# Last stage, slots with experts: TensorE sums the states behind both expert steps, VectorE reads the sums half a slot later, and the closing addition moves to the next slot

## The reference, cut to what matters

```python
x = x + _L1_attn_ref(_layernorm(x), ...)    # recurrence over 32 steps, 512 channels x 16 states
x = x + _L1_ffn_ref(_layernorm(x), ...)     # 8 experts, each 256 -> 512 -> 256
...
    h = dA * h + dBx                        # dA = exp(A * dt), dBx = dt * B_t * x_t
    y = jnp.einsum('bdn,bn->bd', h, C_t) + D * x_t
...
    y = y * jax.nn.silu(z)
    y = y @ out_proj_w.T + out_proj_b       # + residual, layernorm
...
    h = jax.nn.gelu(jnp.einsum('nd,edh->neh', xf, w1) + b1, approximate=False)
    y = jnp.einsum('neh,ehd->ned', h, w2) + b2
    out = (y * norm_g[:, None, None]).sum(axis=1)
```

## Time and profile before

| | us |
|---|---|
| median of 3 runs | 1709.85 (1709.10 to 1711.02) |
| the profiled execution's own time | 1710.99 |
| its span, first to last instruction | 1709.2 |
| last stage with units alone, to the first expert step | about 982 to 1184 |
| last stage, units and experts (40 slots) | about 1184 to 1552 |
| last stage, experts alone | about 1552 to 1704 |
| VectorE busy in the 368 us with both | 342.07 |
| TensorE busy in these 368 us | 311.80 |

### The profile page before, as it was taken

The page is one execution under the profiler, slowest core; times in us unless marked ns, Lnnn a source line. Parts: engine busy times, 40 slices in busy tenths (PEclk is TensorE's granted clock), DMA queues, the critical chain, the costliest instruction groups (busy, mean ns, idle before and its releaser), DMA issues. The chain is left out here.

```text
span 1709.2 us, 33886 instructions
## 1 busy us (share of the span) xinstructions
PE 1373.8 (80%) x12684; PEld 781.7 (46%) x12684; DVE 1221.7 (71%) x2296; ACT 1074.7 (63%) x1902; POOL 772.2 (45%) x842
## 2 busy tenths in 40 slices
PE   5999547978769977877783578995888888799898
PEld 4544223655444435555552223341444445446566
DVE  3599799962348856777765698989999899893100
ACT  1577345543354447777773367876988798894553
POOL 2255000000043434343430077767888788885433
PEclk8999767989869978888895789996999899899999
DMA  6398200000106757776732397877985475460000
GB/s 255 138 352 315 105 0 0 1 1 0 70 32 228 204 109 134 130 127 127 125 62 53 76 246 199 227 217 183 223 187 123 112 177 132 111 149 1 6 8 13
DMA packets 152695, 211.88 MB, mean 124 GB/s; under 512 B 107247, under 2 KB 112303, under 8 KB 139600
## 3 DMA queue, kind: packets, MB, share of 16 engines
q1 hardware_dynamic: 152532, 209.70, 47.5%
HBM read 154.85 MB, written 31.75 MB: 109 GB/s over the span
## 5 line engine op out<-in xcount | busy, mean ns | idle before, releaser
L2865 POOL TENSOR_TENSOR c_st<-c_st,c_c_rep 128x1024 f32<-128x1024 f32 x128 | 301.5, 2356 | 128.1 <-DVE c_st L2978 128.1
L2978 DVE TENSOR_TENSOR_SCAN c_st<-mf_dA,mf_u_ps 128x512 f32<-128x512 f32 x256 | 310.3, 1213 | 2.6 <-ACT mf_dA L3090 2.6
L2806 PE MATMUL mf_eh<-c_early,c_experts 128*128 128x512 f16 x768 | 197.3, 395 | 26.8 <-POOL c_early L2884 15.6
L2888 POOL TENSOR_TENSOR c_early<-c_early 128x512 f16<-128x512 f32 x128 | 149.1, 1166 | 112.0 <-ACT c_early L3107 111.9
L2827 PE MATMUL mf_ey<-c_experts,c_early 128*128 128x256 f16 x1536 | 192.7, 277 | 0.0
L2972 DVE TENSOR_TENSOR mf_u_ps<-c_st,mf_b_ps 128x512 f32<-128x512 f32 x256 | 177.6, 694 | 11.3 <-DVE c_st L2978 0.5
L2827 PEld LDWEIGHTS mf_ey<-c_experts,c_early 128*128 128x128 f16 x1536 | 152.3, 99 | 50.1 <-issue 5.5
L3104 ACT ACTIVATE c_early<-mf_eh,c_vecs 128x512 f16<-128x512 f32 x128 | 88.0, 687 | 118.6 <-PE mf_eh L2806 118.1
L3090 ACT ACTIVATE mf_dA<-c_dt,c_neg_a 128x496 f32<-128x496 f32 x256 | 160.3, 697 | 0.7
L2732 PE MATMUL mf_y_ps<-c_st,c_consts 128*32 128x512 f32 x512 | 107.5, 649 | 59.6 <-POOL c_st L2865 36.4
L259 POOL TENSOR_TENSOR c_parts<-mg_ln_hT,c_parts 128x512 f16<-128x512 f32 x8 | 9.1, 1155 | 297.0 <-ACT c_parts L250 296.9
(11 more groups left out here) (546 smaller groups left out, 2771.0 us busy)
## 6 DMA issues: line engine op xcount, KB each, us to landing
c_st<-xs SPq DMA_DIRECT2D x64, 1024.0 KB, 7.2
a_ctx_t<-in_ctx_t SPq DMA_DIRECT2D x16, 1024.0 KB, 9.3
a_ctx_n<-in_ctx_n SPq DMA_DIRECT2D x16, 1024.0 KB, 8.2
cqs<-a_whole_rows SPq DMA_DIRECT2D x16, 512.0 KB, 6.9
mo_raw<-in_l_w SPq DMA_DIRECT2D x16, 512.0 KB, 4.2
ws<-mo_split SPq DMA_DIRECT2D x32, 256.0 KB, 2.6
c_cq<-cqs SPq DMA_DIRECT2D x16, 512.0 KB, 5.3
c_experts<-ws SPq DMA_DIRECT2D x32, 256.0 KB, 8.4
```

The lines of the kernel that those rows point to most:

```text
L2806: m = e.matmul(bank("hidden", n)[:, :], w1[q][w][:, j, f * P:(f + 1) * P], parts[b % 2][x][:, j, :], start=(j == 0 and w + x == 0), stop=( ...
L2865: e.tensor_tensor(half(u, h), half(u, h), over(c_rep[u // UNITS % 2][:, :], [P, 2, BT], 1), ALU.mult).then_inc(hcs("done"), 1)
L2888: e.tensor_tensor(hid[n % HIDS][1][:, :], g[n % 2][:, :], hid[n % HIDS][0][:, :], ALU.subtract).then_inc(los("done"), 1)
L2978: e.tensor_tensor_scan(st[u % RING][:, j, :], dA[:, n % AHEAD, :], u_ps[j % 2][:, :], 0.0, ALU.mult, ALU.add).then_inc(hs("done"), 1)
```

## The change

Nothing is computed otherwise; four things change their place, all in the slots with expert steps (from s = 24 on):

1. TensorE does `sums(s - 1)` behind both expert steps of its slot, no longer between them.
2. VectorE does `finish` behind the third tile of its slot, no longer behind the first.
3. GpSimd does `gate` behind `weigh(s, 1)`, no longer before it (in all slots).
4. VectorE does `final` of the block before behind the first tile of slot p = 8, no longer behind the third tile of slot p = 7.

```diff
@@ TensorE
-                if 1 <= s <= N:
+                if 1 <= s < FIRST + DELAY:
                     sums(s - 1)
...
                 for n in steps[1:]:
                     hidden(n)
                     if n >= LAG:
                         combine(n - LAG)
+                if FIRST + DELAY <= s <= N:
+                    sums(s - 1)
                 if p == 0:
                     project(b, 0)
                     project(b, 1)
@@ GpSimd
                 for n in steps[:1]:
                     low(n)
-                if 0 <= s - 5 < N and (s - 5) % 4 == 0:
-                    gate((s - 5) // 4)
                 if p == 2:
                     add(b)
                 if s < N:
                     weigh(s, 1)
+                if 0 <= s - 5 < N and (s - 5) % 4 == 0:
+                    gate((s - 5) // 4)
                 for n in steps[1:]:
                     low(n)
@@ VectorE
-                    if j == 0 and 0 <= s - 5 < N and (s - 5) % 4 == 0:
+                    if j == (0 if s < FIRST + DELAY else 2) and 0 <= s - 5 < N and (s - 5) % 4 == 0:
                         finish((s - 5) // 4)
...
-                    if p == DELAY + 1 and j == 2 and b > 0:
+                    if p == DELAY + 2 and j == 0 and b > 0:
                         final(b - 1)
```

## The result

| | before | after |
|---|---|---|
| median of 20 runs each | 1713.32 us | 1708.05 us |
| lowest, highest | 1701.21, 1722.06 | 1695.53, 1717.06 |
| ratio of the times | | 0.9963, 95% interval 0.9945 to 0.998 |
| profiled execution: span | 1709.2 | 1702.2 |
| of it from the first scan of the last stage to the end | 725.7 | 718.4 |

The change makes the kernel 0.37% faster, 6.3 us of 1710 (interval 3.4 to 9.4); the two medians differ by 5.3. The forecast was 12.7 by its sum. The direction was right, the size was twice the measured one. The forecast time of 1697.5 missed the median of 1708.05 by 10.6 us, of which 3.5 come from the starting point: the kernel before has a median of 1713.3 over 20 runs, not the 1709.85 of the first three.

What follows compares the result with a forecast made beforehand. VectorE was taken to set the pace of the 40 slots, TensorE that of the tail. Gains of 3.3 + 3.3 + 1.8 + 1.7 = 10.1 us plus 2.6 at the end made 12.7, forecast 1697.5 us, range 1691 to 1708.5.

Steps and rivals of the forecast that it cites:

- Both waits of slots 41 and 57: VectorE's `finish` and `final` waits in slots 41 and 57 shrink, 3.8 us gained in each slot before later fetches.
- the ring: State buffers for units 44 and 60 come back later behind the delayed sums; 0.5 us lost at each.
- `gate`'s move: GpSimd's `gate` behind `weigh` costs nothing new; 0 to 1.3 us per slot either way, hidden by TensorE's wait.
- The step at the end: In slot 64 the second expert step lies before the last sums, so TensorE's tail is 2.6 us shorter.
- the price of late sums: Sums and the fetches behind them come later in the 40 slots; put at nothing, given slack in the ring.
- Cost 0: Later `finish` delays sums in every fourth slot; slack covers it, with 0 to 3 us per place as bounds.
- the residual waits: Slots 34 and 50: the projection starts up to 2.6 us earlier and both residual waits go, 1.7 us gained.
- The 3.7 are absorbed: TensorE's 3.7 us delay from late `finish` fits a group of four slots: 25.2 us of work against VectorE's 36.8.
- the z waits of slots 29 and 33: `finish` comes 3.7 us of scans later, covering most of its z transfer wait; 1.8 of 2.5 us gained.
- A: Rival: stalls only move, VectorE waits for states in three or four slots a block; 4.3 us left, 1705.5; chance 0.15.
- B: Rival: late `finish` makes TensorE the bound, at the half clock; 9 us slower, 1719; chance 0.14.

Runs made afterwards that it cites:

- run 4: The changed kernel with GpSimd's `gate` ahead of `weigh(s, 1)` again; ratio 0.9962 to the kernel before.
- run 5: The kernel before with one operand of VectorE's 15 small routing operations in PSUM, routing weights left out of the result; ratio 0.9976 to the kernel before.
- run 2: The kernel before with only TensorE's sums moved behind both expert steps from slot 24 on; ratio 0.9982 to the kernel before.
- run 3: The changed kernel with `sums(s - 1)` back between the two expert steps in all slots; ratio 0.9969 to the kernel before.
- run 11: The kernel before with run 5's edit of the small operations and only `final` moved half a slot later; ratio 0.9962 to the kernel before.
- run 1: The changed kernel with the x and z rows' transfers issued ahead of the states' fetch from slot 24 on; ratio 0.9929 to the kernel before.
- run 7: The kernel of run 1 with run 5's edit of the small operations; ratio 0.9889 to the kernel before.
- run 6: The changed kernel with run 5's edit of the small operations; ratio 0.9915 to the kernel before.
- run 8: Run 7 with sums between the expert steps again in slots 25, 41, 57 and `finish` after the first scan in slots 33, 49; ratio 0.987 to the kernel before.

## Why the prediction was half right

**Right.** Both waits of slots 41 and 57 went as the replay said, and further: forecast -3.8 each before the ring, ledger -5.5 and -4.7. The excess is a premise that erred to the good side: I let the turn and `rest` come as before, but in slot 39 the second transpose followed TensorE's first after 0.5 us and not after 2.4, and `hidden` ran at 1333.34, 1.7 earlier than at 1335.02. TensorE in the changed kernel:

```profile
1333.34 2.52 PE L2806 MATMUL mf_eh<-c_early,c_experts 128*128 128x512 f16 x6 [1.89 <-POOL c_early L2886]
1335.66 2.14 PE L2827 MATMUL mf_ey<-c_experts,c_early 128*128 128x256 f16 x12
...
1340.33 1.06 PE L2732 MATMUL mf_y_ps<-c_st,c_consts 128*32 128x512 f32 x8
```

That first step also took 4.3 us, where it had taken 5.2 at a granted clock of 0.50. The sums then ended at 1341.4, not 1344.0. Why the second transpose came sooner is open. `gate`'s move costs nothing that run 4 could see.

The step at the end: last scan to end is 2.4 us shorter, forecast 2.6. This stretch varies from 152.8 to 165.8 us over the fourteen profiles, so the pair of times does not prove it; what TensorE has left does. From the end of GpSimd's last `weigh` to the end, before and after:

```profile
1553.50:1709.20 155.70, 144.26 (x948) 96.93 (x946) 14.08 (x48) 72.87 (x111) 64.38 (x54) 0.97 0.02 8
1548.90:1702.20 153.30, 141.82 (x930) 95.31 (x928) 14.08 (x48) 72.30 (x110) 64.39 (x55) 0.97 0.02 8
```

TensorE has 18 matmuls less, one expert step, at the same clock. Runs 5 and 2, without and with late sums, show the same: 155.9 and 153.2 us.

**The step that failed** is the price of late sums, put at nothing. The prediction gave the z rows' transfer one sentence, for slots 29 and 33, and then set the delayed sums in all other slots to "Cost 0", since the ring of states had 3 us of slack. But SyncE's list is in order: a transfer that needs nothing of the sums stood behind a fetch that does. In slots 45 and 61, where it had not been last, it now costs 2.2 and 2.8 us, and in 41 and 57 it takes over the wait of `finish` when TensorE is already done. For slot 45 the issue was 2.5 us later than in the kernel before, and the wait is 2.2. Late sums are not the whole cause, for VectorE's lead counts too. With sums in their old place a late `finish` meets no such wait in these two slots (run 3); an early one does, once VectorE comes sooner (run 11, 2.59 and 2.86). Moving the transfers alone removed the waits: 5.8 us in run 1, which also had 8.7 us less of small operations in its profile, and 4.5 in run 7 against run 6, where these are alike.

**Mis-sized.** The ring at units 44 and 60: taken as 0.5 each, measured 1.4 and 1.8. The mechanism was the one described, sums behind a step with `bias` that waits for `final`: in run 8, with those sums between the steps, the waits in slots 43 and 59 are gone. Here too VectorE's lead is the other half: in run 2 the sums are as late, but VectorE asks for unit 44 at 1363.9 and not at 1359.3, and there is no such wait.

**Also wrong: the residual waits** (forecast -1.7, measured +0.6). With late sums and `finish` early they went, as the term said (run 2); the late `finish` brought them back. The projection of slot 34 stands behind the sums of the next group, which wait for the late `finish`. TensorE in the changed kernel:

```profile
1269.00 1.93 PE L2732 MATMUL mf_y_ps<-c_st,c_consts 128*32 128x512 f32 x8 [5.61 <-DVE mf_xq L2988]
1270.87 2.09 PE L2806 MATMUL mf_eh<-c_early,c_experts 128*128 128x512 f16 x6
...
1277.80 7.17 PE L2777 MATMUL mf_eh<-mf_w_out,mf_gz 128*128 128x256 f32 x32
```

5.61 us of waiting, then sums of 1.93 where others take 1.07: the half clock (1.2 GHz) for a while, the granted clock 0.80 over 1264 to 1272 where the kernel before has 1.00. The projection starts 0.6 earlier, as much as the whole kernel stands ahead. "The 3.7 are absorbed" holds over a group, and not where a projection follows in the next slot.

**Closed by the ledger**, VectorE's path: forecast -10.1; slots 41 and 57 better by 2.6; z rows in 45 and 61, +5.0; states +2.2; all else, together +2.8 (forecast -3.5, ledger -0.7: residual waits, the z waits of slots 29 and 33, the two new ones ahead of slot 24, and 0.8 us more of small operations in slots 28 and 30); small operations in slots 44, 46, 60 and 62, -2.2. That makes -4.9, as seen between first and last scan. The small operations are in no term of the prediction: 13 us of waiting that the profile calls busy. Between these two profiles they cancel nearly (16.3, 14.9), so by the profiles they do not explain the miss. By the times they may hide part of the gain: with them out of both kernels the change was worth 10.5 us, with 6 on either side.

**The rivals.** A had the right shape, stalls that only move, and even came near in size (4.3 left, 6.3 measured); but it named states in three or four slots a block, and it is the z rows more than the states. That it came near in size is luck: its sum gave back terms that were in fact won (slots 41 and 57) and kept one that was not (the residual waits). Run 11 is its pure case. B did not happen as a bound: TensorE's wait for `finish` grew to 20.7 us (25 forecast), the mean clock fell from 0.95 to 0.93, and the price that can be seen was the residual wait.

## What to carry to other kernels

When work moves later on one engine, list every entry that stands behind its waiters in the in-order lists, not only the waiters: a DMA issue that needs nothing of the moved work is delayed with it, and issuing it one list entry earlier was worth some 4.5 us here (runs 6 and 7, whose intervals overlap), where the whole change was worth 6.3. Replay to the next two or three waits after each stall removed; a stall that vanishes without the next transfer coming earlier can reappear there nearly in full (run 11). And look at the spread of durations of small equal instructions before trusting a busy share: busy time can be waiting.

## What the hardware showed unasked

A 128 x 32 operation of VectorE with both inputs in SBUF took 0.17 to 2.3 us, and where it was long it ended with GpSimd's running operation; with one input in PSUM its group means were 0.16 to 0.19 in each kernel looked at. The product of `enter` (128 x 512, one input in PSUM) took 0.67 to 0.70 in all 254 that follow the first scan of the stage, whatever GpSimd did. A 256 KB transfer issued behind a 1024 KB one took 10.4 us to be seen by its reader, the large one 6.7.
